# A two-layer graph network on one core: joining four partial tables by pieces in the last stage, and moving four groups of edges from the first layer's pass to the second's

## The reference

```python
h = relu(layernorm(x));  x = x + L0(h)
h = relu(layernorm(x));  x = x + L1(h)

# L0, a weighted graph convolution: w_norm = dinv[row] * w * dinv[col]
out = segment_sum(w_norm[:, None] * (h @ kernel)[col], row)      # relu(out + bias)

# L1, messages along each edge in both directions
msg_fwd  = concat([H[heads], E]) @ W_fwd  + b_fwd
msg_back = concat([H[tails], E]) @ W_back + b_back
agg = segment_sum(messages) / (count + 1e-7)
y   = where(agg >= 0, agg, 0.01 * agg) + H
out = gamma * (y - mean(y)) * rsqrt(var(y) + 1e-5) + beta
```

## Time and profile before

| | us |
|---|---|
| median of 3 runs | 4114.44 (4105.33 to 4119.76) |
| the profiled execution's own time | 4114.12 |
| its span | 4112.3 |
| TensorE busy in the span | 3375.8 (82%) |
| GpSimd busy | 3005.9 (73%) |
| VectorE busy | 2882.9 (70%) |
| ScalarE busy | 1844.9 (45%) |
| mean granted TensorE clock | 0.932 |

### The profile page before, as it was taken

How to read it: one execution, slowest core, us unless ns; L and a number is a source line. 1 busy time by engine, 2 the same in 40 slices (tenths; PEclk the granted TensorE clock), 3 DMA queues, 4 the chain that set the end, 5 groups by cost and what they waited for, 6 DMA issues and landing times. The chain is left out here.

```text
span 4112.3 us, 100240 instructions
## 1 busy us (share of the span) xinstructions
PE 3375.8 (82%) x30528; PEld 2831.5 (69%) x30528; DVE 2882.9 (70%) x7843; ACT 1844.9 (45%) x4477; POOL 3005.9 (73%) x1814
## 2 busy tenths in 40 slices
PE   3455699889898888898954899999999999899966
PEld 3454687777777777777734677777777777777746
DVE  9899887777787777877746666565656565656515
ACT  1040455555555555555534344444444444444424
POOL 5778688888888888888832888777777777778611
PEclk9787899999999999999976799999999999999988
DMA  9980787878787877877786555545554555555592
GB/s 168 275 264 16 159 146 136 146 136 144 137 147 134 146 135 142 142 140 138 130 182 171 84 87 83 83 78 82 81 81 80 81 81 82 80 82 82 88 151 81
DMA packets 708626, 502.02 MB, mean 122 GB/s; under 512 B 283653, under 2 KB 620074, under 8 KB 708084
## 3 DMA queue, kind: packets, MB, share of 16 engines
q0 software_dynamic: 257584, 174.71, 37.6%
q1 hardware_dynamic: 450376, 320.42, 29.1%
q10 hardware_dynamic: 124, 0.05, 0.0%
HBM read 282.86 MB, written 238.48 MB: 127 GB/s over the span
## 5 line engine op out<-in xcount | busy, mean ns | idle before, releaser
L1733 POOL DMA_INDIRECT gcn_sums<-shared,ds_to_i x784 | 1312.3, 1674 | 482.4 <-ACT shared L1986 256.5
L879 POOL DMA_INDIRECT gcn_sums<-fl_sums,fl_to_i x832 | 1364.6, 1640 | 293.1 <-DMA gcn_sums<-fl_sums,fl_to_i 155.8
L1941 PE MATMUL bank<-ds_counts,ds_parts 128*128 128x256 bf16 x3675 | 604.4, 277 | 0.0
L2010 ACT COPY ds_turned<-bank 128x1024 bf16<-128x1024 bf16 (+1 forms) x325 | 313.1, 963 | 578.8 <-PE bank L1926 426.3
L1107 ACT COPY fl_sums<-bank 128x256 f32<-128x256 f32 x832 | 313.0, 376 | 557.4 <-PE bank L1034 289.3
L1974 ACT CAST ds_counts<-bank 128x392 bf16<-128x392 f32 x800 | 383.2, 490 | 219.2 <-PE bank L1885 179.1
L1961 PE MATMUL bank<-ds_turned,ds_now 128*128 128x512 bf16 (+1 forms) x1950 | 458.7, 372 | 0.0
L1870 DVE TENSOR_TENSOR src_sums<-src_sums,bank 128x512 f32<-128x512 f32 (+1 forms) x325 | 213.1, 656 | 280.3 <-PE bank L1961 275.2
L1905 PE MATMUL bank<-shared 128*128 128x128 f32 x1568 | 368.6, 319 | 46.0 <-DVE shared L1800 22.2
L917 DVE SCALAR_TENSOR_TENSOR fl_same<-fl_key_b,fl_pat,bank 128x128 f32<-128x128 bf16 x832 | 276.0, 344 | 161.1 <-PE bank L1034 132.2
L1033 PE MATMUL bank<-fl_pay,fl_same 128*128 128x128 f32 x1664 | 335.0, 283 | 48.2 <-issue 35.3
(11 more groups left out here) (275 smaller groups left out, 6988.3 us busy)
## 6 DMA issues: line engine op xcount, KB each, us to landing
fl_attrs<-in_edge_attr SPq DMA_DIRECT2D x104, 512.0 KB
shared<-in_edge_attr SPq DMA_DIRECT2D x194, 256.0 KB
fl_rel_b<-offset_rows SPq DMA_DIRECT2D x104, 256.0 KB
fl_key_b<-key_rows SPq DMA_DIRECT2D x104, 256.0 KB
gcn_sums<-zeros SPq DMA_DIRECT2D x40, 640.0 KB
shared<-key_rows SPq DMA_DIRECT2D x98, 256.0 KB
gcn_sums<-fl_sums,fl_to_i POOLq DMA_INDIRECT x832
near<-src_float SPq DMA_DIRECT2D x1, 12892.0 KB
```

Of the source, the lines that this page charges most:

```text
L879: nc.gpsimd.indirect_dma_start(out=d.tab_gcn[j % K], out_offset=bass.IndirectOffsetOnAxis(ap=to_i[:, (GPI * kk + gi) % 4, j:j + 1], axis=0 ...
L1733: nc.gpsimd.indirect_dma_start(out=d.tab_gcn[j % K].rearrange("n (two f) -> (n two) f", two=2), out_offset=bass.IndirectOffsetOnAxis(ap=to ...
L1941: ins = nc.tensor.matmul(row_bank[:, 0:2 * P], parts[:, tile, s, :], counts[:, h, tile, :, :].rearrange("p b q -> p (b q)"), start=(tile = ...
```

## The change

- `first_layer` has 100 groups instead of 104: slots 0, 1, 2 and 25 (`LIGHT`) hold 3 groups, the others 4. In a slot with 3 groups the blocks and the pair batches are spread over 24 steps instead of 32 (`turn_at`, `pairs_at`). Ring positions follow the group's number (`in_ring`).
- `dense_sums` has 102 groups instead of 98: a prologue of 4 groups (before 6), 4 groups beside each of tiles 0 to 23 (before 0 to 22), and 2 beside tile 24 (before none). The join of the tables is gone from it; GpSimd waits only for the last scatters.
- `last_nodes` joins the tables: for each of the 5 pieces SyncE loads table 0 into `src_attr` and tables 1 to 3 into part buffers, and VectorE adds them. The adds of piece r+1 stand in the VectorE order at steps 3, 4, 5 of piece r; those of piece 0 come before the first tile. TensorE's first transpose of a piece waits for its adds. `h1` and `x1` are loaded into rings of 3 and 4 pieces, which adds waits on SyncE.
- beta is added in `gcn_nodes`: GpSimd writes `x1 + beta` of each finished piece to a new buffer of two pieces, and that is stored as `x1`. `last_nodes` has no such adds.
- `load_sums` (a path that these inputs don't take) loses its own join.

```diff
-G1 = GPI * 2 * DS
+LIGHT = (0, 1, 2, 2 * DS - 1)
+G1 = GPI * 2 * DS - len(LIGHT)
 NB = NG - G1
 GL = 4
-PG = 6
-BT = (NB - PG) // GL
+PG = 4
+GL_LAST = NB - PG - GL * (SUPER - 1)
...
+        def groups_in(i, kk):
+            if not isinstance(i, int):
+                return GPI
+            k = 2 * i + kk
+            return 0 if k == 2 * DS else GPI - 1 if k in LIGHT else GPI
...
+        def steps(i, kk):
+            return J * (groups_in(i, kk) or GPI)
+        def turn_at(i, kk, c):
+            return [b for b in range(BLOCKS + 1) if b * steps(i, kk) // BATCHES == c]
+        def pairs_at(i, kk, c):
+            return [n for n in range(BATCHES) if (2 * n + 1) * steps(i, kk) // (2 * BATCHES) == c]
...
 # gcn_nodes
+        def _(pool):
+            pool.wait_ge(beta_in, 16)
+            for r in range(PIECES):
+                pool.wait_ge(x1_ready, PT * (r + 1))
+                if r >= 2:
+                    pool.wait_ge(x1_stored[r % 2], 16 * (r // 2))
+                nc.gpsimd.tensor_tensor(x_beta[:, r % 2, :, :], piece(x, r), beta[:]..., ALU.add).then_inc(beta_added, 1)
...
 # dense_sums
-        def loop(eng, pair_of_tiles, between=None):
-            pair_of_tiles(0, 0, True, False)
-            pair_of_tiles(0, 1, True, False)
-            with eng.Fori(1, BT // 2) as i:
-                pair_of_tiles(i, 0, True, False)
-                pair_of_tiles(i, 1, True, False)
-            pair_of_tiles(BT // 2, 0, True, False)
-            if between:
-                between()
-            pair_of_tiles(BT // 2, 1, False, False)
-            pair_of_tiles(SUPER // 2, 0, False, True)
+        def loop(eng, tile):
+            tile(0, 0, False)
+            tile(0, 1, False)
+            with eng.Fori(1, SUPER // 2 - 1) as i:
+                tile(i, 0, False)
+                tile(i, 1, False)
+            tile(SUPER // 2 - 1, 0, False)
+            tile(SUPER // 2 - 1, 1, False)
+            tile(SUPER // 2, 0, True)
...
-            pool.wait_ge(first_in, 16)
-            for k in range(1, K):
-                if k > 1:
-                    pool.wait_ge(merged, 16 * (k - 1))
-                nc.gpsimd.dma_start(d.src_attr[:], d.table(k), accum_op=ALU.add).then_inc(merged, 16)
-            pool.wait_ge(merged, 16 * (K - 1))
+            for k in range(K):
+                pool.wait_ge(added[k], 16 * (J // K) * NB)
...
 # last_nodes
+            def load_tables(r):
+                sp.dma_start(piece(d.src_attr, r), piece(d.table(0), r)).then_inc(acc_in[r], 16)
+                for k in range(1, K):
+                    n = r * ADDS + k - 1
+                    if n >= PB:
+                        sp.wait_ge(table_added, n - PB + 1)
+                    sp.dma_start(part[n % PB], piece(d.table(k), r)).then_inc(part_in[n % PB], 16)
...
+            load_tables(0)
             for m, a in enumerate((d.w_back[F:2 * F, :], ...)):
                 sp.dma_start(w[:, m, :], a).then_inc(w_in, 16)
             load(0)
...
             for r in range(1, PIECES):
+                load_tables(r)
                 load(r)
...
+            def add_table(r, k):
+                n = r * ADDS + k
+                if k == 0:
+                    dve.wait_ge(acc_in[r], 16)
+                dve.wait_ge(part_in[n % PB], 16 * (n // PB + 1))
+                if k > 0:
+                    dve.wait_ge(table_added, n)
+                nc.vector.tensor_tensor(piece(d.src_attr, r), piece(d.src_attr, r), part[n % PB], ALU.add).then_inc(table_added, 1)
+            for k in range(ADDS):
+                add_table(0, k)
             for t in range(NT + 2):
                 by_count(t)
                 bend(t - 1)
                 add_up(t - 2)
                 r, at = divmod(t, PT)
+                if 3 <= at < 3 + ADDS and r + 1 < PIECES:
+                    add_table(r + 1, at - 3)
...
             def turn(t):
+                if t % PT == 0:
+                    pe.wait_ge(table_added, ADDS * (t // PT + 1))
```

More of the change, by code:

```diff
@@ L844, in slot @@
                 k = 2 * i + kk
-                for gi in range(0 if last else GPI):
-                    g, h = group(i, kk, gi), gi % 2
+                for gi in range(groups_in(i, kk)):
+                    g, h = group(i, kk, gi), in_ring(i, kk, gi) % 2
                     at_least(sp, to_ready, g - 1)
@@ L1072, in slot @@
                 first = isinstance(i, int) and i == 0
-                for c in range(C):
+                for c in range(steps(i, kk)):
                     gi, j = divmod(c, J)
@@ L1078, in slot @@
                         spread(i, kk, gi, 1)
-                    if j == U + 1 and not last and not (ends_groups(i, kk) and gi == GPI - 1):
+                    if j == U + 1 and not last and not (ends_groups(i, kk) and gi == groups_in(i, kk) - 1):
                         spread(i, kk, gi + 1, 0)
-                    at, b = c % STRIDE, c // STRIDE
-                    if not first and at == 0 and b < BLOCKS:
-                        turn(k, kk, b)
-                    if not first and at == 0 and 1 <= b <= BLOCKS:
-                        product(i, kk, b - 1)
-                    if not last and at == 1 and b < BATCHES:
-                        pairs(k, b)
+                    for b in turn_at(i, kk, c):
+                        if not first and b < BLOCKS:
+                            turn(k, kk, b)
+                        if not first and b > 0:
+                            product(i, kk, b - 1)
+                    for n in pairs_at(i, kk, c):
+                        if not last:
+                            pairs(k, n)
             loop(pe, slot)
@@ L1133, in slot @@
                         make_pay(i, kk, gi, 1)
-                    if j == U + 1 and not last and not (ends_groups(i, kk) and gi == GPI - 1):
+                    if j == U + 1 and not last and not (ends_groups(i, kk) and gi == groups_in(i, kk) - 1):
                         make_pay(i, kk, gi + 1, 0)
-                    at, b = c % STRIDE, c // STRIDE
-                    if not first and at == 0 and b < BLOCKS:
-                        keep_turned(k, kk, b)
-                    if not last and at == 1 and b < BATCHES:
-                        keep_pairs(k, kk, b)
+                    for b in turn_at(i, kk, c):
+                        if not first and b < BLOCKS:
+                            keep_turned(k, kk, b)
+                    for n in pairs_at(i, kk, c):
+                        if not last:
+                            keep_pairs(k, kk, n)
             loop(act, slot)
@@ L1430, in _ @@
             store_h1(PIECES - 1)
-            sp.wait_ge(stored, 16 * 2 * PIECES)
+            sp.wait_ge(stored, 16 * PIECES)
+            for b in range(2):
+                sp.wait_ge(x1_stored[b], 16 * len(range(b, PIECES, 2)))
+        @block.gpsimd
+        def _(pool):
[4 more added lines that the diff above has]
+                    pool.wait_ge(x1_stored[r % 2], 16 * (r // 2))
+                nc.gpsimd.tensor_tensor(x_beta[:, r % 2, :, :], piece(x, r), beta[:].unsqueeze(1).to_broadcast([NP, PT, F]), ALU.add).then_inc(beta_added, 1)
         @block.vector
@@ L1851, in _, with add @@
             dve.wait_ge(src_zeroed, CHUNKS)
-            def add(i, h, beside, last):
+            def add(i, h, last):
                 t = 2 * i + h
@@ L1911, in _, with products @@
                     pairs(0, 0, c, first=True)
-            def products(i, h, beside, last):
+            def products(i, h, last):
                 t = 2 * i + h
@@ L1932, in products @@
                     ahead = [] if last else list(range(3 * b, min(3 * b + 3, BATCHES)))
-                    steps = list(steps_of(b)) if beside else []
+                    steps = list(steps_of(i, h, b))
                     for k in range(wide(b)):
@@ L1996, in _, with copies @@
             keep_now(0, 0)
-            def copies(i, h, beside, last):
+            def copies(i, h, last):
                 t = 2 * i + h
@@ L2120, in load_sums @@
         sem = semaphores(nc, ctx, "load_")
[L2121 to L2122 removed]
+        loaded = sem("loaded")
         block = ctx.enter_context(nc.Block())
@@ L2158, in last_nodes @@
         PIECES = NT // PT
+        ADDS = K - 1
+        PB = 2 * ADDS
+        spare_words = d.places[:].rearrange("p m t q -> p (m t q)").bitcast(F32)[0:NP, 0:2 * PT * F]
+        own_parts = sb("part", [NP, PB - 2, PT, F])
+        part = [own_parts[:, b, :, :] for b in range(PB - 2)] + [spare_words[:, b * PT * F:(b + 1) * PT * F].rearrange("p (t f) -> p t f", f=F) for b in range(2)]
         row_sums = sb("row_sums", [F, ROWS])
-        h1 = sb("h1", [NP, NT, F])
-        x1 = sb("x1", [NP, NT, F])
+        H1_RING, X1_RING = 3, 4
+        h1 = sb("h1", [NP, H1_RING, PT, F])
+        x1 = sb("x1", [NP, X1_RING, PT, F])
         count_rows = sb("count_rows", [P, ROWS])
@@ L2212, in _ @@
             nc.gpsimd.memset(count_rows[:, ROWS // 2:], 0.0).then_inc(rows_zeroed, 1)
-            pool.wait_ge(bias_in, 32)
-            for r in range(PIECES):
```

(2 more changed lines are left out.)

146 lines of the change are left out of this document (65 added, 81 removed).

## The result

The changed kernel takes 4142.76 us (median of 5 runs, 4134.94 to 4154.08) against 4114.44 before. The ratio is 1.0076, 95% interval 1.0061 to 1.0091: slower, where the prediction said 4083 and faster. Its profiled execution took 4134.94 us (span 4132.8), the quickest of its five, so what follows accounts for 20.5 of the 28 us.

What follows compares the result with a forecast made beforehand. GpSimd's scatters were taken to bound the first layer, VectorE the node stage, TensorE the tiles, and no single full engine the last stage. -59 + 11.6 + 1 + 15 = -31.4 against 4114.1 gave 4083 us, range 4061 to 4105.

Steps and rivals of the forecast that it cites:

- Step 1: First layer: four groups less shorten GpSimd's queue, taken as the limit; -59 us, bounds -64 and -30.
- D: First layer: slots with a group less still last 58.1 us; -30 instead of -59, total 4112; chance 6%.
- B: Node and last stages: GpSimd's add doesn't hold VectorE's adds, last-stage adds half hidden; -11.6 and -6, total 4065; chance 15%.
- Step 2: Node stage: GpSimd's beta adds hold VectorE's adds for four pieces, 2.9 us each; +11.6, bounds 0 and +14.5.
- Step 3: Second layer's prologue: two groups fewer, VectorE carrying its end; -19.1 us, bounds -16 and -23.
- Step 4: Tiles 22 to 24: six more groups beside tiles 23 and 24, 4.8 us each; +31.5, bounds 25 and 45.
- Step 5: End of second layer: merges leave the 24.6 us gap, 4.1 stays; +1 for the whole layer, -8 to +14.
- Step 6: Last stage: joining tables adds a later start, waits and VectorE adds, less GpSimd's holds; +15, bounds +4 and +35.
- E: Last stage: becomes bound by its table loads, 209 us instead of 124; total 4153; chance 5%.
- C: Last stage: TensorE's clock at 1.2 GHz throughout, a piece 30.7 us; +20, total 4103; chance 13%.

Runs made afterwards that it cites:

- e3: The kernel before with the eighth scatter of every first-layer group left out (104 of 832), for measuring alone: 4094.49 us, ratio 0.9951.
- e9: The kernel before with both layers' loops written out and the eighth scatter of every first-layer group left out, for measuring alone: 3923.11 us, ratio 0.9551.
- e10: The changed kernel with both layers' loops written out on TensorE, VectorE and ScalarE: 4020.44 us, ratio 0.9784 to the kernel before.
- e1: The kernel before with 145 never executed ScalarE instructions added, putting its tile loop at the changed kernel's place: 4139.58 us, ratio 1.006.
- e6: The kernel before with the second layer's loop over pairs of tiles written out on TensorE, VectorE and ScalarE: 4059.1 us, ratio 0.9866.
- e7: The changed kernel with the second layer's loop over pairs of tiles written out on TensorE, VectorE and ScalarE: 4058.35 us, ratio 0.9868.
- e15: The changed kernel with never executed instructions moving the second layer's ScalarE and TensorE loops back to their earlier places: ratio 1.0019 to the kernel before.
- e4: The kernel before with only beta moved to the node stage: 4102.21 us, ratio 0.997.
- e5: The kernel before with beta in the node stage and the tables joined in the last stage, its groups unchanged: 4110.27 us, ratio 0.9994.
- e2: The changed kernel with 111 never executed ScalarE instructions added, putting its tile loop back at its earlier place: 4136.99 us, ratio 1.0052 to the kernel before.
- e13: The changed kernel with never executed instructions moving the second layer's ScalarE, VectorE and TensorE loops back to their earlier places: ratio 1.0028 to the kernel before.

## Why the prediction was wrong

- **Step 1 failed, in its premise.** "832 x 1.99 = 1658 is the whole stage" was true, and GpSimd did set the end of the stage; that nothing else stood close behind was not. By e3, an eighth of the scatters away, the next limit came after 24 us. So the four groups were priced at all of their 63.7 us of queue. The slots' rows read 65.6 and 60.8 in turn; I averaged them to 63.2, found GpSimd's 63.7 and stopped. Equal scatters don't explain times that alternate. What alternates is the loop, and TensorE's chain through its branch came to the same 126 us a pair. -26.5 came instead of -59, and e9 and e10 show the second limit. Slots 1 and 2 took 53.2 and 54.7 us and not 51, nor D's 58.1; that D's -30 lies near the -26.5 is chance. B falls too: the adds are held.
- **No step had the tiles.** Adding no work to a loop was priced at nothing. But the loop's place moved, on three engines, and cost 25 us (e1 shows it in the kernel before, e6 and e7 by having no loop). It is the larger part of the 0.8%, but without it no gain is left either: e15, with ScalarE's and TensorE's places put back, is at 1.0019 (1.0006 to 1.0032).
- **Step 2 held**: +10.7 on VectorE against 11.6; the stage shows +4.9 in the changed kernel, where its first add came 5.5 us sooner, and +11.7 in e4.
- **Step 3 held**: -17.9 against -19.1. **Step 4** was too dear: +23.5 against +31.5 and under its bound of 25, mostly tile 23 (62.3 us against 66) and tile 24 (39.4 against 43.8): 3.9 us a group, about its products, and not 4.8. **Step 5** held for the merges: e5's gap is 7.0 us instead of 25.5. The changed kernel's is 17.6 where 9.5 + 4.1 = 13.6 was forecast.
- **Step 6** had +15 and got +19.1. The pieces are right. The start was 3.5 us short: the first result waits for gamma, whose load I did not count, behind four tables, four weights and three loads in SyncE's queue. Of the rivals, E (loads) is refuted, and so is C in its size: the pieces keep the forecast 24 us, though the clock is lower than in the earlier trace rows (the stretch at 0.50 in each of pieces 1 and 2 grew from 6.8 to 10.2 us; C had it throughout). Two windows of the changed kernel's last stage, the loads at 298 GB/s and the pieces behind them:

```profile
4020.00:4040.00 20.00, 13.86 (x107) 12.91 (x108) 14.35 (x54) 5.74 (x29) 0.00 (x0) 0.97 1.14 298
...
4080.00:4100.00 20.00, 13.88 (x88) 13.40 (x88) 10.95 (x40) 6.02 (x22) 0.00 (x0) 0.74 0.10 28
```

So -31.4 became +20.5 in the profiled executions: 32.5 from step 1, 25.1 from tiles 0 to 21 (all but 4 of it the code's place, by e15), 4.1 from step 6, and -10 from the others. The 8 us more of the medians have no place in a trace.

## What to carry to other kernels

Times that alternate with a loop's turns point to a second limit, however well their mean fits a queue: take the shortest slot as what the engines can do, and price a cut as the smaller of the two limits' gains. A change ahead of a long loop moves its code; look behind the branch back on each engine, in the kernel before too, and write the loop out where the stall stands on TensorE's chain, before anything finer is judged. In a chain of loads, count every load that the first consumer waits for, the small ones too.

## What the chip showed beyond that

- A stall of 3 to 6 us at a branch back also cost the clock: it was granted at 0.50 for some microseconds behind each of the nine branches. Written out, ten tiles lost 17 us of idle time and 16 us of busy time (e6).
- ScalarE's loop of 296 instructions ran without a fetch when it began at 2 or 108 modulo 128 (before, e2, e13 to e15; e3) and with some five a turn at 19 (after, e1). Other places were not tried, so what makes a place good is open.
- TensorE's instruction packets are of 16 KB (292 packets, 4.78 MB on the page of before), those of the small engines' queue of 8 KB (250, 2.05 MB). Straight code was fetched without a visible stall, over more than 10,000 instructions on TensorE.
